# Two batches' projections moved to other steps in front of the 16-wide attention stages

## The chip, the cores and the metric

One core of a Trainium2 chip runs the whole kernel in one launch. The metric is device time in microseconds (us) for that launch. The engines are TensorE (PE, with its weight loads listed as PEld), VectorE (DVE), ScalarE (ACT), GpSimd (POOL) and SyncE (SP), which here only issues DMAs. "SPq" and "ACTq" are the DMA issues of SyncE and ScalarE.

## The reference

Eight layers act on x of shape (8, 256, 256), each as x + layer(layernorm(x)), in the order attention, FFN, attention, FFN and so on. The attentions read a second input ctx of the same shape. Layers 0 and 6 are the ones that the change touches. Both are the same computation with their own weights, 16 heads of width 16:

```python
qh = (q @ Wq.T + bq).reshape(B, Nq, 16, 16).transpose(0, 2, 1, 3)    # q = layernorm(x)
kh = (k @ Wk.T + bk).reshape(B, Nkv, 16, 16).transpose(0, 2, 1, 3)   # k = v = ctx
vh = (v @ Wv.T + bv).reshape(B, Nkv, 16, 16).transpose(0, 2, 1, 3)
attn = jax.nn.softmax(jnp.einsum('bhqd,bhkd->bhqk', qh, kh) * 0.25, axis=-1)
out = jnp.einsum('bhqk,bhkd->bhqd', attn, vh)
out = out.transpose(0, 2, 1, 3).reshape(B, Nq, 256) @ Wo.T + bo
```

The layers between them (a routed FFN, a 64-wide attention, a second FFN, an attention without heads, a quantised FFN) and the last layer (a block-quantised linear) are other functions of the kernel, which the change leaves alone.

## The kernel before, in words

`narrow_head_attention` (line 591) is called twice, as stage a0 and as stage a6. In the trace the names of both begin with `a_`: a0 lies at about 8 to 230 us of the span, a6 at about 1605 to 1840 us.

The work is cut into 64 pairs of heads, 8 for each of the 8 batches. A loop over a step number T is unrolled in each engine's program, from -14 to 87 or so; a pair's scores are computed at step T and its second, "shifted" scores at step T + 7 (`LAG`), where t = T - 7. Every engine walks through the same steps in the same order:

- PE at step T: first half of `scores_and_shifted` (line 776: one head's scores of pair T into `ps_s`, one head's shifted scores of pair t into `ps_t`), then the rounds that the list `EVENTS` (line 622) gives for T (`project`, line 726), then the second half, then at every second step the product with the values (`weighted_values`, line 807).
- DVE at step T: the maxima over the scores (`largest`, line 875), between its two halves its share of the rounds of step T - 1 (`read_round`), and for batch f at T = 8f - 14 the normalisation's statistics and at 8f - 13 its application (line 910 and 916), which waits for POOL's reciprocal root (`norm_rstd`, line 60).
- ACT at step T: its share of the rounds of step T - 1, `context_high(f)` at T = 8f - 9 (line 1033), then the exponentials of pair t (line 999), whose results PE waits for one step later, since the bank of shifted scores must be read before it is written again (line 792). The maxima go into the operand of the shifted scores by DMAs that ACT issues (`place_maxima`, line 972).
- SP: `place_unit(u)` (line 707), one for each unit of 4 pairs. It issues 6 DMAs for q and 6 for k of 64 KB, which lay the high and low parts of q and k out as the operands `qa` and `ka`. Unit 2f and 2f + 1 belong to batch f. PE waits for unit u at step T = 4u (line 783). `context(f)`, 2 DMAs that fetch a batch of ctx, stands in the same queue: `context(2)` right behind `place_unit(2)`, before `place_unit(3)` (line 719 to 722).
- POOL: a loop over the batches f: `norm_rstd(f)`, `context_low(f)`, `output_bias(f - 1)`, in this order (line 1074).

A round is one use of one of three PSUM banks: "hT" transposes the normalised input of a batch, "q", "k" and "v" are its projections (12 matmuls of 128 x 256 each), "mT", "OT", "BT" and "out" are transposes of maxima and outputs and the output projection. A round claims its bank once the round three places before it in the sorted list is consumed. The context's parts `ctx_hi` and `ctx_lo` have one buffer: `context_high(f)` waits until the values of batch f - 1 are projected (line 936).

Of the kernel before, what the change touches and what calls it, by code (L numbers as in the profile page):

```python
# [590 lines left out]
def narrow_head_attention(nc, chip, stage, w, prefetch, late=(), x_rest=()):  # L591
# [28 lines left out]
    STATS, APPLY, CTX = -14, -13, -9  # L620
    FIRST = STATS
    EVENTS = []
    for f in range(B):
        EVENTS += [(8 * f - 10, 0, "hT", f), (8 * f - 8, 0, "q", f), (8 * f - 6, 0, "k", f), (8 * f - 2, 1, "v", f), (8 * f + 20, 3, "out", f)]
    for u in range(NUNIT):
        EVENTS += [(4 * u + 4, 2, "mT", u), (4 * u + LAG + 6, 2, "OT", u), (4 * u + LAG + 8, 2, "BT", u)]
    EVENTS.sort()
# [4 lines left out]
    def rounds_at(s):  # L632
        return [(kind, n) for at, o, kind, n in EVENTS if at == s]

    def group_at(s):

        n, odd = divmod(s - LAG - PPG, PPG)
        return n if not odd and 0 <= n < NG else None

    with ExitStack() as ctx:  # L640
# [84 lines left out]
        def _(pe):  # L725
            def project(kind, n):
# [10 lines left out]
                elif kind in "qkv":  # L737
                    if n == 0:
                        pe.wait_ge(sem["W_lo"], "qkv".index(kind) + 1)
                    _, hi, lo = weights[kind]  # L740
                    if kind == "q":
                        pe.wait_ge(sem["hT_lo"], n + 1)
# [183 lines left out]
        def _(act):  # L926
            def weights_high(kind):
                W, hi, lo = weights[kind]
                if kind == "q":
                    nc.scalar.activation(hi[:, :, :], W, ACT.Copy, scale=SCALE).then_inc(sem["W_hi"], 1)  # L930
                else:
                    nc.scalar.copy(hi[:, :, :], W).then_inc(sem["W_hi"], 1)

            def context_high(f):
                act.wait_ge(sem["ctx"], 16 * KC * (f + 1))
                after(act, sem["vp"], f)
                nc.scalar.copy(ctx_hi[:, :, :], ctxT[:, :, :]).then_inc(sem["ctx_hi"], 1)
# [34 lines left out]
            def place_maxima(u, t):  # L972

                part, name = (m_hi, "m_hi") if t == 0 else (m_lo, "m_lo")
                act.wait_ge(sem[name], u + 1)
                if t == 0 and u >= RING:
                    act.wait_ge(sem["st"], 2 * PPU * (u - RING + 1))
                for i in range(2):
                    row = i * HALF + K1 + t
                    act.dma_start(qa[row:row + 1, u % RING, :, :].bitcast(F32),  # L980
                                  part[i * PPU:(i + 1) * PPU, u % 2, :].bitcast(F32)).then_inc(sem[f"mrow{u % 2}"], 16)
# [11 lines left out]
            def keep_output(n):  # L993

                act.wait_ge(sem["pv"], n + 1)
                after(act, sem["OTp"], (n - NO) // 2 + 1)
                nc.scalar.copy(osb[:, n % NO, :], ps_o[:, :]).then_inc(sem["osb"], 1)

            def exponentials(t, i):

                act.wait_ge(sem["st"], 2 * t + (1 - i) + 1)
                after(act, sem["pv"], (t - NPT) // PPG + 1)
                nc.scalar.activation(probT[:, t % NPT, i, :, :], ps_t[i][:, :, :], ACT.Exp).then_inc(sem["exp"], 1)  # L1003

            def read_round(kind, n):
                if kind == "hT":
                    hT_high(n)
                elif kind in "qk":
                    high_part(kind, n)
                elif kind == "v":  # L1010
                    keep_v(n)
                elif kind == "mT":
                    maxima_high(n)
                elif kind == "BT":
                    keep_oT(n)
# [7 lines left out]
            for T in range(FIRST, LAST + 1):  # L1023
                t = T - LAG
                if T == STATS:
                    weights_high("q")
                if T == APPLY:
                    weights_high("k")
                    weights_high("v")
                for this in rounds_at(T - 1):  # L1030
                    read_round(*this)
                for f in range(B):
                    if T == 8 * f + CTX:
                        context_high(f)
                if 0 <= t < NT:
                    exponentials(t, 1)
                for kind, n in rounds_at(T - 1):
                    if kind == "mT":
                        place_maxima(n, 0)
                if group_at(T - 1) is not None:  # L1040
                    keep_output(group_at(T - 1))
                if 0 <= t < NT:
                    exponentials(t, 0)
                for kind, n in rounds_at(T - 1):
                    if kind == "mT":
                        place_maxima(n, 1)
                if T == NPAIR:
                    loads = prefetch(act, sem["wload"])
# [1388 lines left out]
def build(nc, a, out):  # L2437
    with ExitStack() as ctx:
# [28 lines left out]
        with ExitStack() as st:  # L2467
# [11 lines left out]
            def _(pool):  # L2479
                nc.gpsimd.memset(chip.minus_half[:, :], -0.5).then_inc(sem["consts"], 1)  # L2480
                pool.wait_ge(sem["consts"], 1)


        stages = [lambda: narrow_head_attention(nc, chip, "a0", w0, fetch1, w0.late, [(chip.x[:, TB:2 * TB, :], x_tiles[:, TB:2 * TB, :]),
                                                                                               (chip.x[:, 2 * TB:, :], x_tiles[:, 2 * TB:, :])]),
                  lambda: expert_choice_ffn(nc, chip, "f1", w1, fetch2),
                  lambda: head_attention(nc, chip, "a2", w2, fetch3),
                  lambda: top2_experts(nc, chip, "f3", w3),
                  lambda: context_attention(nc, chip, "a4", fetch5),
                  lambda: quantised_ffn(nc, chip, "f5", w5, fetch6),  # L2490
                  lambda: narrow_head_attention(nc, chip, "a6", w6, fetch7),
                  lambda: block_quantised_linear(nc, chip, "f7", w7, out)]
        for stage in stages:
# [62 lines left out]
```

## Time and profile before

| | us |
|---|---|
| median of 3 runs | 1927.48 (1919.68 to 1937.14) |
| profiled execution | 1938.52 |
| its span in the trace | 1936.6 |

The span is the time from the first to the last recorded instruction; the rest of an execution's time, 1.9 us, lies around it. The three runs spread over 0.9% with nothing changed between them. All times of rows below are us from the span's start, unless marked ns.

### The profile page before, as it was taken

To read this page: it belongs to the slowest core of one execution; us is meant where nothing else is said; L and a number is where in the kernel's file an instruction comes from. 1 tells how busy PE (TensorE), PEld (TensorE's weight loads), DVE (VectorE), ACT (ScalarE), POOL (GpSimd) and SP (SyncE) were. 2 spreads that over 40 slices of the span, in tenths; PEclk is the share of its full clock that TensorE was granted. 3 is DMA by queue.
4 is the path that set the end of the run, shared out by engine and by line. 5 is a ranking of instruction groups with operands and counts; after the bars stand their busy time and mean duration, and the time that the engine had idled before them with its cause. 6 is when DMAs were issued, how large, how long until landed. Compare 5 with 4: busy or idle time off the path is not lost. (4 is left out here: it accounts for less than half of the span.)

```text
span 1936.6 us, 32029 instructions
## 1 busy us (share of the span) xinstructions
PE 1625.2 (84%) x10798; PEld 1359.1 (70%) x10798; DVE 1260.0 (65%) x2837; ACT 944.8 (49%) x2139; POOL 429.8 (22%) x429
## 2 busy tenths in 40 slices
PE   4899738999995799999999989999985996899815
PEld 3566427888885788988889868889874785666413
DVE  3677355656563878766787568766756754677297
ACT  1566524444343768766687644433433541566400
POOL 2111013656564312211122000000003312111022
PEclk7899879999998999999999989999997996799656
DMA  3322053464654100000000100000024002222001
GB/s 125 112 87 82 29 211 102 121 150 122 149 122 96 60 2 6 5 5 5 0 5 0 66 1 1 1 1 0 1 66 136 1 0 68 76 88 83 9 0 43
DMA packets 81169, 108.35 MB, mean 56 GB/s; under 512 B 13104, under 2 KB 75312, under 8 KB 78512
## 3 DMA queue, kind: packets, MB, share of 16 engines
q1 hardware_dynamic: 64256, 85.33, 13.2%
q0 software_dynamic: 12288, 16.79, 5.0%
q10 hardware_dynamic: 4528, 4.98, 0.8%
q8 instruction: 57, 0.93, 0.2%
q14 instruction: 40, 0.33, 0.1%
HBM read 66.68 MB, written 14.68 MB: 42 GB/s over the span
## 5 line engine op out<-in xcount | busy, mean ns | idle before, releaser
L881 DVE TENSOR_REDUCE a_nmax<-a_s 128x2 f32<-128x512 f32 x256 | 170.2, 687 | 119.4 <-PE a_s L796 118.9
L1003 ACT ACTIVATE a_probT<-a_t 128x512 f32<-128x512 f32 x256 | 151.3, 602 | 146.0 <-PE a_t L800 125.2
L317 PE MATMUL a_o<-a_probT,a_vb 128*128 128x128 f32 x1024 | 143.4, 284 | 28.2 <-ACT a_oT L525 27.5
L574 POOL TENSOR_TENSOR a_k_hi<-a_k_hi,a_k_lo 64x256 fp32r<-64x256 f32 x128 | 93.3, 729 | 328.7 <-ACT a_k_hi L501 319.2
L796 PE MATMUL a_s<-a_ka,a_qa 48*128 48x256 f32 x512 | 125.3, 351 | 39.7 <-DMA a_qa<-a_m_lo 14.9
L317 PEld LDWEIGHTS a_o<-a_probT,a_vb 128*128 128x128 f32 x1024 | 126.6, 194 | 44.6 <-issue 43.3
L796 PEld LDWEIGHTS a_s<-a_ka,a_qa 48*128 48x128 f32 x512 | 81.1, 210 | 99.0 <-issue 72.6
L514 ACT ACTIVATE a_prob<-a_score,a_nmax 128x256 f32<-128x256 f32 x256 | 119.4, 472 | 46.8 <-DVE a_nmax L421 45.5
L421 DVE TENSOR_REDUCE a_nmax<-a_score 128x2 f32<-128x512 f32 x128 | 88.4, 690 | 82.4 <-PE a_score L298 80.6
L800 PE MATMUL a_t<-a_qa,a_ka 50*128 50x256 f32 x512 | 124.2, 343 | 2.2 <-DMA a_qa<-a_m_lo 1.2
L1427 POOL DMA_INDIRECT x_rows<-f_hn,f_scatter_row x64 | 108.7, 1698 | 29.9 <-issue 19.0
L1384 ACT ACTIVATE f_gate<-f_gate 128x512 f32<-128x512 f32 x64 | 38.3, 599 | 150.6 <-PE f_gate L1216 129.2
L2111 PE MATMUL f_y<-area_odd_parts,f_y_hi 128*128 128x256 f32 x384 | 109.2, 284 | 0.0
L2277 ACT ACTIVATE f_relu<-f_u 128x512 f32<-128x512 f32 x96 | 57.2, 598 | 85.3 <-PE f_u L2099 84.8
L1315 DVE TENSOR_TENSOR f_y<-f_gate,f_value 128x512 f32<-128x512 f32 x64 | 44.1, 688 | 81.3 <-PE f_value L1216 81.3
L520 ACT COPY a_probT<-a_T 128x512 f32<-128x512 f32 x128 | 75.6, 590 | 41.5 <-PE a_T L306 38.6
L1228 PE MATMUL f_z<-area_odd_parts,f_y_hi 128*128 128x256 f32 x384 | 84.7, 287 | 9.0 <-DVE f_y_lo L1307 9.0
L63 POOL TENSOR_TENSOR a_rstd<-a_veps,minus_half 128x2 f32<-128x2 f32 x32 | 22.9, 716 | 305.7 <-DVE a_veps L57 305.7
L63 POOL TENSOR_TENSOR f_rstd<-f_veps,minus_half 128x4 f32<-128x4 f32 x12 | 12.1, 1011 | 345.5 <-DVE f_veps L57 345.5
L2209 DVE TENSOR_TENSOR f_y<-f_relu 128x512 f32<-128x512 f32 x96 | 65.1, 690 | 34.8 <-ACT f_relu L2277 32.1
L800 PEld LDWEIGHTS a_t<-a_qa,a_ka 50*128 50x128 f32 x512 | 78.2, 201 | 10.6 <-issue 5.1
L428 DVE TENSOR_SCALAR a_prob<-a_prob,a_rinv 128x256 f32<-128x256 f32 x256 | 80.2, 356 | 4.5
(329 smaller groups left out, 5080.8 us busy)
## 6 DMA issues: line engine op xcount, KB each, us to landing
area_odd<-in_L_experts SPq DMA_DIRECT2D x15, 1536.0 KB, 7.7
a_ctxT<-in_ctxT SPq DMA_DIRECT2D x64, 128.0 KB, 2.5
a_qa<-a_q_hi SPq DMA_DIRECT2D x128, 64.0 KB, 2.6
a_ka<-a_k_hi SPq DMA_DIRECT2D x128, 64.0 KB, 2.6
area_odd<-in_L_W SPq DMA_DIRECT2D x2, 3072.0 KB, 11.0
a_qa<-a_q_lo SPq DMA_DIRECT2D x64, 64.0 KB, 2.6
a_ka<-a_k_lo SPq DMA_DIRECT2D x64, 64.0 KB, 2.6
x_rows<-x_tok SPq DMA_DIRECT2D x1, 2048.0 KB, 7.6
```

The costliest lines, as they stand in the source:

```text
L317: last = nc.tensor.matmul(ps_o[:, :], vb[:, kc, hh[i] * P:(hh[i] + 1) * P], probT[:, u % 2, kc, i, :], start=(i == 0 and kc == 0), stop=(i ...
L421: nc.vector.tensor_reduce(nmax[:, u % NPROB, :], ps_score[u % NB][:, :, :], AX.X, ALU.max, negate=True).then_inc(sem["nmax"], 1)
L428: last = nc.vector.tensor_scalar(prob[:, u % NPROB, i, :], prob[:, u % NPROB, i, :], rinv[:, u % NPROB, i:i + 1], None, ALU.mult)
L514: last = nc.scalar.activation(prob[:, u % NPROB, i, :], ps_score[u % NB][:, i, :], ACT.Exp, bias=nmax[:, u % NPROB, i:i + 1], accum_out=rs ...
L574: nc.gpsimd.tensor_tensor(k_hi[other, h, :], k_hi[own, h, :].bitcast(F32), k_lo[own, h ^ 1, :].bitcast(F32), ALU.add).then_inc(sem["k_copy ...
L796: last_s = nc.tensor.matmul(ps_s[i][:, half, :], qa[rows, u % RING, j, half * P:(half + 1) * P], ka[rows, u % RING, j, :], start=True, sto ...
L800: last_t = nc.tensor.matmul(ps_t[o][:, half, :], ka[rows, v % RING, m, half * P:(half + 1) * P], qa[rows, v % RING, m, :], start=True, sto ...
L881: nc.vector.tensor_reduce(nmax[:, u % 2, :, i * PPU + j], ps_s[i][:, :, :], AX.X, ALU.max, negate=True).then_inc(sem["nmax"], 1)
L1003: nc.scalar.activation(probT[:, t % NPT, i, :, :], ps_t[i][:, :, :], ACT.Exp).then_inc(sem["exp"], 1)
L1228: last = nc.tensor.matmul(ps_z[s // 2][:, s % 2, :], h[:, f, s * P:(s + 1) * P], W[:, f, :], start=(f == 0 and i == 0), stop=(f == NF - 1 ...
L1427: nc.gpsimd.indirect_dma_start(chip.x_rows, bass.IndirectOffsetOnAxis(ap=scatter_row[:, q, s:s + 1], axis=0), z[:, q, s, :], None, compute ...
L2111: last = nc.tensor.matmul(ps_y[t // 2][:, t % 2, :], h[:, e % 2, f, t * P:(t + 1) * P], W, start=(f == 0 and i == 0), stop=(f == NF[e] - 1 ...
```

## The change

For batch 1, the q round goes from step 0 to step 4, the k round from step 2 to step 5. For batch 0, the v round goes from step -2 to step 2. `context_high(1)`, which must stand behind the values of batch 0, goes from step -1 to step 3. Since the rounds are sorted by step and then by a rank (q, k: 0; v: 1; mT: 2), the list around them goes from hT1, v0, q1, k1, mT0, hT2, v1 to hT1, v0, q1, mT0, k1, hT2, v1. Nothing else is edited, and it holds for both stages.

```diff
@@ -621,7 +621,8 @@
     for f in range(B):
-        EVENTS += [(8 * f - 10, 0, "hT", f), (8 * f - 8, 0, "q", f), (8 * f - 6, 0, "k", f), (8 * f - 2, 1, "v", f), (8 * f + 20, 3, "out", f)]
+        EVENTS += [(8 * f - 10, 0, "hT", f), (8 * f - 8 if f != 1 else 4, 0, "q", f), (8 * f - 6 if f != 1 else 5, 0, "k", f),
+                   (8 * f - 2 if f != 0 else 2, 1, "v", f), (8 * f + 20, 3, "out", f)]
     for u in range(NUNIT):
         EVENTS += [(4 * u + 4, 2, "mT", u), (4 * u + LAG + 6, 2, "OT", u), (4 * u + LAG + 8, 2, "BT", u)]
@@ -1030,7 +1031,7 @@
                 for f in range(B):
-                    if T == 8 * f + CTX:
+                    if T == (8 * f + CTX if f != 1 else 3):
                         context_high(f)
```

## Rows read from the trace of the kernel before

**Rows 1.** The page's busy time of one engine: us, share of the span, instructions.

```profile
PE 1625.2 (84%) x10798; PEld 1359.1 (70%) x10798; DVE 1260.0 (65%) x2837; ACT 944.8 (49%) x2139; POOL 429.8 (22%) x429
```

**Rows 2.** Windows: stretch, its length, busy us (instructions) by engine, granted PE clock, DMA.

```profile
core 0: us, PE busy (x) PEld busy (x) DVE busy (x) ACT busy (x) POOL busy (x), PEclk, DMA share, GB/s
31.60:52.70 21.10, 17.74 (x68) 14.19 (x68) 11.86 (x26) 2.63 (x6) 1.63 (x3) 0.50 0.26 85
52.70:81.20 28.50, 22.26 (x161) 15.35 (x160) 15.51 (x33) 12.53 (x26) 3.37 (x4) 0.74 0.40 130
1625.50:1646.65 21.15, 17.79 (x68) 14.22 (x69) 11.86 (x26) 2.63 (x6) 1.79 (x3) 0.50 0.27 90
1646.65:1675.30 28.65, 25.11 (x161) 17.59 (x160) 15.56 (x33) 13.64 (x27) 3.34 (x4) 0.62 0.24 75
```

**Rows 3.** Timeline of PE in a0: start, us, instruction, count [idle before, releaser].

```profile
31.57 0.76 PE L796 MATMUL a_s<-a_ka,a_qa 48*128 48x256 f32 x2 [2.94 <-DMA a_ka<-a_k_lo]
...
46.17 3.01 PE L796 MATMUL a_s<-a_ka,a_qa 48*128 48x256 f32 x8
...
55.10 0.35 PE L796 MATMUL a_s<-a_ka,a_qa 48*128 48x256 f32 x1 [0.29 <-DVE a_nmax L881]
```

**Rows 4.** Timeline of PE in a6, steps 0, 2, 8, 14 and 22.

```profile
1625.49 0.76 PE L796 MATMUL a_s<-a_ka,a_qa 48*128 48x256 f32 x2 [2.81 <-DMA a_ka<-a_k_lo]
...
1631.94 0.79 PE L752 MATMUL a_proj<-a_ctx_hi,a_Wk_hi 128*128 128x256 f32 x2
...
1634.80 0.80 PE L796 MATMUL a_s<-a_ka,a_qa 48*128 48x256 f32 x4
...
1649.91 0.35 PE L796 MATMUL a_s<-a_ka,a_qa 48*128 48x256 f32 x1 [1.18 <-ACT a_probT L1003]
...
1675.25 0.39 PE L796 MATMUL a_s<-a_ka,a_qa 48*128 48x256 f32 x1
...
1697.33 0.38 PE L796 MATMUL a_s<-a_ka,a_qa 48*128 48x256 f32 x1
```

**Rows 5.** Timeline of SP's issues in a0: q and k of unit 2, then the context.

```profile
38.04 1.19 SPq L704 DMA_DIRECT2D a_qa<-a_q_hi  x2
...
40.55 1.23 SPq L704 DMA_DIRECT2D a_qa<-a_q_hi  x2
44.94 2.46 SPq L704 DMA_DIRECT2D a_ka<-a_k_hi  x4
...
48.96 2.30 SPq L694 DMA_DIRECT2D a_ctxT<-in_ctxT  x2
```

**Rows 6.** The context tile, us from issue to landing: first in a0, then in a6.

```profile
DMA to landing us min/median/max: 3.3/3.5/3.7
...
DMA to landing us min/median/max: 2.5/2.7/3.0
```

**Rows 7.** Timeline of ACT in a0, step 7.

```profile
53.40 0.62 ACT L937 CAST a_ctx_hi<-a_ctxT 128x512 fp32r<-128x512 f32 x1
53.98 0.60 ACT L1003 ACTIVATE a_probT<-a_t 128x512 f32<-128x512 f32 x1
```

**Rows 8.** Timeline of ACT in a6, step 7.

```profile
1647.24 0.62 ACT L937 CAST a_ctx_hi<-a_ctxT 128x512 fp32r<-128x512 f32 x1
1647.88 1.28 ACT L1003 ACT_TABLE_LOAD   x1
1649.17 1.09 ACT L1003 ACTIVATE a_probT<-a_t 128x512 f32<-128x512 f32 x2
```

**Rows 9.** Timeline of DVE in a0, steps 1 to 4.

```profile
37.15 0.87 DVE L856 SCALAR_TENSOR_TENSOR a_q_lo<-a_proj,area_even,a_q_hi 128x256 fp32r<-128x256 f32 x2
...
41.70 0.69 DVE L881 TENSOR_REDUCE a_nmax<-a_s 128x2 f32<-128x512 f32 x1 [2.48 <-PE a_s L796]
...
43.45 0.69 DVE L881 TENSOR_REDUCE a_nmax<-a_s 128x2 f32<-128x512 f32 x1
...
45.43 0.73 DVE L70 TENSOR_SCALAR a_hn<-x_tok,a_mv,a_rstd 128x256 f32<-128x256 f32 x2
```

**Rows 10.** Timeline of POOL in a0: context's low part, output bias, reciprocal root.

```profile
29.90 1.26 POOL L1068 TENSOR_TENSOR a_ctx_lo<-a_ctxT,a_ctx_hi 128x512 fp32r<-128x512 f32 x1 [5.14 <-ACT a_ctx_hi L937]
31.12 1.41 POOL L1062 TENSOR_TENSOR x_tok<-x_tok,area_even 128x256 f32<-128x256 f32 x2
...
43.61 0.71 POOL L63 TENSOR_TENSOR a_rstd<-a_veps,minus_half 128x2 f32<-128x2 f32 x1 [11.09 <-DVE a_veps L57]
```

## Prediction

> **What bounds the kernel now.** I read the page first: PE is busy 84% of the span, more than any other engine [rows 1]. That is an average over eight stages; the change lives in the head of two of them, so I read those heads by stretches [rows 2]. In a0 the steps 0 to 6 (first scores up to the last matmuls without shifted scores) take 21.1 us, in a6 21.15 us, both at a granted clock of 0.50, which is the lower of TensorE's two levels, 1.2 GHz. The next eight steps (to the second half of step 14) take 28.5 and 28.65 us at mean clocks of 0.74 and 0.62. Later a batch of eight steps at full clock takes 1697.33 - 1675.25 = 22.1 us [rows 4]. So the head costs more per step than the rest, and half clock and waits are the two reasons.
>
> Then I read the timelines of each queue through steps 0 to 8, because the change moves rounds between queues that are in order. I set x = 0 at the first scores (31.57 in a0, 1625.49 in a6 [rows 3, 4]). Step 8 began at x = 23.5 in a0 and 24.4 in a6 [rows 3, 4]. In a6 the PE had waited 1.18 us for ACT's exponential there, and that exponential stood behind `context_high(2)` and a table load of 1.28 us [rows 8]; in a0 it also ran right behind `context_high(2)`, but no later than PE wanted it [rows 7]. That order on ACT is the thing to keep in mind: at step 7 ACT first takes the third batch of ctx and only then can read the first shifted scores.
>
> **What the change moves.** Nothing is added or removed: the same 36 matmuls for q1, k1 and v0, the same DVE, ACT and POOL work, the same DMAs, in another order. Everything follows from three shifts.
>
> *v0 from step -2 to step 2.* A projection at half clock costs 2.86 us of PE (1634.80 - 1631.94 [rows 4]). At step -2 it was covered by the wait for the placed operands (2.94 us idle in a0, 2.81 in a6 even after it [rows 3, 4]), so taking it away there gains nothing: step 0 is set by the DMAs of unit 0, and those by q0 and k0, which stay. At step 2 it lies where k1 lay, with the same price.
>
> *context_high(1) from step -1 to step 3.* POOL is in order, and `norm_rstd(2)`, for which DVE waits at step 3, stands behind `context_low(1)` and `output_bias(0)`. Both were long done; now they begin when v0 is projected. By rows: v0 ends at x = 6.4; ACT keeps v and casts ctx by 7.6 (two instructions of 0.6 [rows 7]); POOL needs 1.26 + 1.41 + 0.71 us [rows 10], to x = 11.0. DVE reaches that point at x = 10.3 (below). The new wait is 0.7 us; behind it stands the first maximum of step 4.
>
> *q1 and k1 from steps 0 and 2 to 4 and 5.* On PE the sum for steps 0 to 6 changes only by v0, 2.86 us, of which most fills gaps that PE has there (21.1 - 17.7 = 3.4 us idle [rows 2]). But q1 and k1 feed SP, and that queue has hardly any room. Working forward at half clock:
> - Two bare steps take 3.1 us (8 matmuls in 3.01 [rows 3]), so step 2 begins at 3.1, v0 runs from 3.6 to 6.5, the second maximum of step 2 begins at 7.35. The statistics follow and the next maximum begins 43.45 - 41.70 = 1.75 later [rows 9], at 9.1; the step's other maximum ends at 10.4, the application (0.73 [rows 9]) waits until 11.05 and ends at 11.8.
> - q1 runs on PE from 10.4 to 13.2, the transposes of the maxima take about 0.5 more; two maxima of step 4 and 5 then end at 15.85, and the low part of q1 (0.87 [rows 9]) is done at x = 16.65. Before, it was done at 38.02 - 31.57 = 6.5.
> - SP then issues q of unit 2. Six transfers take 40.55 + 1.23 - 38.04 = 3.74 us, the six for k 48.96 - 44.94 = 4.0 with the gaps [rows 5]. The low part of k1 is done at about 20.4, just as SP gets to it. So unit 2 is issued by x = 24.4 (before: 17.4), and the two DMAs of `context(2)` behind it by about 25.7. The second lands 2.7 us (a6) to 3.5 us (a0) after its own issue begins at 25.0 [rows 6]: x = 27.7 and 28.5. Before, it had landed by the time ACT came.
> - ACT at step 7 would be ready for it at about x = 22.6 and waits some 5 us. Queued behind it on ACT are all exponentials. The cast of 0.62 and the exponential of 0.60 [rows 7] give PE's step 8 in a0 at x = 29.7; with the 1.28 of the table load, which stands behind the cast [rows 8], in a6 at x = 30.3. Unit 2 itself lands at about 26.5, so it is hidden by this wait.
> - Unit 3 is issued by x = 33.4 and needed at step 12, which was at about 39 and is now later: hidden.
>
> Step 8 comes 29.7 - 23.5 = **6.2 us later in a0** and 30.3 - 24.4 = **5.9 us later in a6**. Behind step 8 the same work remains with PE the fullest engine, so I expect none of it back.
>
> **The clock.** In both stages before, the mean clock is 0.50 up to the start of step 7 and above it from there on, in a0 more (0.74) than in a6 (0.62) [rows 2]: behind the dense v1 it rose for a while. Now PE is idle for over 6 us between steps 7 and 8, and I take it to be at half clock for step 8's q2, 2.86 us. At full clock that is half, so a0, which had more of it, loses 1.4 and a6, where it held for less, some 0.5. The bounds: 0 in each if it has risen anyway; at most 2.5 in a0. I don't take more, since a6 went through these eight steps no slower than a0 although its clock was lower (28.65 and 28.5 [rows 2]): waits cover much of it.
>
> The Trainium skill, "TensorE: Matmul & The Clock Gate", Part 1, "What's actually happening", says that the clock is low by default and that activity releases it. By that rule packing q1, k1, v1 in front of the shifted scores should raise the clock earlier; that is the second rival below. The rows only show that a projection alone at steps 0 and 2 did not raise it and v1 did [rows 2].
>
> **Sum.** 6.2 + 5.9 + 1.4 + 0.5 = 14.0 us on the profiled execution's 1938.5, that is 0.72%. On the median shown, 1927.5, which is 0.6% below the profiled one, it gives 1941.4.
>
> **Rivals.**
> 1. *Slower by over 1%.* The stall leaves the clock low for more than step 8: if the eight steps after it, at present 28.5 us, or the next eight, run at half clock throughout. Eight steps take 22.1 us at full clock [rows 4] and about 28.6 at mostly half clock [rows 2], so each further batch at half clock costs 6.5 us in one stage. With one such batch the sum is +20.5 (1947.9). It decides from the point where the second batch's steps (14 on) stay at 0.5. Against: the clock rose at step 14 in both stages, and the dense hT3 and v2 are still there.
> 2. *Not slower: the packing does what it seems to be for.* If the clock rises during k1 or v1 and is high from step 8 to 14, these 6.5 steps take 17.9 us (6.5/8 x 22.1) instead of 25.3 (1675.25 - 1649.91 [rows 4]), which gives 7.4 back in each stage. The sum is 12.1 - 14.8 = -2.7, 1924.8. For: the eight steps do take 28.5 now. Against: the ACT wait comes between the packed rounds and those steps, and leaves PE idle for longer than the wait of 2.9 us before step 0, after which steps 0 to 6 ran at 0.50.
> 3. *The delay is smaller.* If q1 itself runs at full clock and POOL is not late, the low part of q1 comes at about x = 14.5 and each stage loses 2 us less: +10.0, 1937.4. I count it to the forecast.
>
> **How the numbers follow.** Forecast, +8 to +19 us: 0.70. Rival 1: 0.18. Rival 2 and everything else near zero: 0.12. The three runs before spread by 0.9%, so about 1% is what a measurement tells from no change; my forecast of 0.72% lies within it but near the edge, so a quarter of its upper half may be read as slower by over 1%. Chances: slower by over 1% 0.25, within 1% 0.72, faster 0.03. The range takes the forecast's bounds (+8 to +19) with 0.3% of scatter on the upper side, and reaches down to rival 2's side to no change: 1928 to 1953.
>
> **What would show it.** In the changed kernel's timeline: ACT's `a_ctx_hi` of step 7 with an idle stretch of some 5 us before it, ended by a DMA of `a_ctxT`; SP's q of unit 2 issued 16 to 17 us after the first scores; POOL's third `a_rstd` right behind `output_bias`, and a wait of DVE for it under 1.5 us; PE's step 8 at x = 29 to 31. The stretch of steps 0 to 6 should still be about 22 us at 0.50. I am wrong if step 8 comes at x below 27, if ACT finds the context landed, or if the clock is 1.00 through steps 8 to 13.

## The result, and the profile after

The changed kernel is slower: 1943.92 us median of 4 runs (1939.18 to 1947.70) against 1923.89 (1919.68 to 1937.14), ratio 1.0092 with a 95% interval of 1.0055 to 1.0130. (The two medians alone would give 1.0104, the means of the runs, 1943.7 and 1926.2, give 1.0091.) Measured again beside the last experiments it was 1.0077 (1.0050 to 1.0104). So it loses 0.8 to 0.9%, some 15 to 18 us.

The two profiled executions don't show that in their spans (1937.4 and 1936.6 us), because the one of before (1938.52 us) was slower than all of its timed runs and the one of after the fastest of its four. What they show is where the time goes in the two heads. I use x again, the time since a stage's first scores; they are at 31.15 in a0 and 1629.27 in a6. First PE's timeline of the changed kernel, in the columns of [rows 3]:

```profile
31.15 0.80 PE L797 MATMUL a_s<-a_ka,a_qa 48*128 48x256 f32 x4 [4.72 <-DMA a_ka<-a_k_lo]
...
50.75 0.50 PE L797 MATMUL a_s<-a_ka,a_qa 48*128 48x256 f32 x2
...
61.43 0.55 PE L797 MATMUL a_s<-a_ka,a_qa 48*128 48x256 f32 x1 [8.73 <-ACT a_probT L1004]
...
62.15 0.79 PE L753 MATMUL a_proj<-a_hT_hi,a_Wq_hi 128*128 128x256 f32 x2
...
1629.27 0.80 PE L797 MATMUL a_s<-a_ka,a_qa 48*128 48x256 f32 x4 [4.63 <-DMA a_ka<-a_k_lo]
...
1661.12 0.55 PE L797 MATMUL a_s<-a_ka,a_qa 48*128 48x256 f32 x1 [10.29 <-ACT a_probT L1004]
```

Step 8 begins at x = 30.3 in a0 and 31.8 in a6, where [rows 3, 4] gave 23.5 and 24.4. In front of it PE stands idle for 8.7 and 10.3 us, and what ends the idle time is ACT's exponential. So the next timeline is ACT's, at step 7, first in a0, then in a6 (compare [rows 7, 8]):

```profile
50.98 0.61 ACT L964 COPY a_vb<-a_proj 128x512 f32<-128x512 f32 x1
60.17 0.62 ACT L938 CAST a_ctx_hi<-a_ctxT 128x512 fp32r<-128x512 f32 x1 [8.58 <-DMA a_ctxT<-in_ctxT]
60.69 1.08 ACT L1004 ACTIVATE a_probT<-a_t 128x512 f32<-128x512 f32 x2
...
1658.45 0.62 ACT L938 CAST a_ctx_hi<-a_ctxT 128x512 fp32r<-128x512 f32 x1 [8.72 <-DMA a_ctxT<-in_ctxT]
1659.09 1.28 ACT L1004 ACT_TABLE_LOAD   x1
```

ACT waited 8.6 us for the third batch's context, with the exponentials behind it. The context is late because of SP's queue (a0, beside [rows 5]):

```profile
48.18 1.57 SPq L705 DMA_DIRECT2D a_qa<-a_q_hi  x2
49.80 1.67 SPq L705 DMA_DIRECT2D a_qa<-a_q_lo  x2
51.51 1.23 SPq L705 DMA_DIRECT2D a_qa<-a_q_hi  x2
52.78 2.50 SPq L705 DMA_DIRECT2D a_ka<-a_k_hi  x4
55.33 1.23 SPq L705 DMA_DIRECT2D a_ka<-a_k_lo  x2
56.60 1.06 SPq L695 DMA_DIRECT2D a_ctxT<-in_ctxT  x2
```

The queue stands still until q1's low part is done (x = 17.0; before 6.5), then issues 12 transfers and only then the two of the context. They land 2.5 to 2.9 us after their issue. Last the windows, for a0 and a6: steps 0 to 6 up to the end of v1, as in the first and third of [rows 2]; the idle stretch before step 8; steps 8 to 14.

```profile
core 0: us, PE busy (x) PEld busy (x) DVE busy (x) ACT busy (x) POOL busy (x), PEclk, DMA share, GB/s
31.15:50.75 19.60, 16.85 (x80) 13.80 (x80) 11.33 (x25) 3.14 (x8) 3.29 (x4) 0.58 0.12 41
52.60:61.40 8.80, 0.10 (x2) 0.00 (x1) 1.49 (x3) 1.23 (x3) 0.54 (x1) 0.60 0.36 119
61.40:86.90 25.50, 24.22 (x150) 16.45 (x150) 13.02 (x29) 10.64 (x23) 2.82 (x4) 0.54 0.39 136
1629.27:1648.57 19.30, 16.54 (x80) 13.48 (x81) 11.24 (x24) 2.82 (x7) 3.29 (x4) 0.59 0.13 44
1650.70:1661.10 10.40, 0.13 (x4) 0.01 (x1) 1.37 (x3) 2.62 (x4) 1.96 (x3) 0.55 0.36 119
1661.10:1681.20 20.10, 17.02 (x150) 12.27 (x150) 12.93 (x29) 10.54 (x23) 1.38 (x2) 0.89 0.26 81
```

Two things are to be seen. With the projections packed the clock of the head was higher, 0.58 and 0.59 instead of 0.50 (0.72 and 0.59 in a second trace, run 12): steps 0 to 7 are done by x = 21.5, before by 23.2, with one projection more in them. And it bought nothing, since the next 9 to 10 us are idle.

### The profile page after: what moved, and what is told of

The parts are those of the page before. It is cut to its first block and busy times, and to the rows that moved or that the text cites. A ratio compares the mean times of both kernels' runs of the same rounds, so it can differ in the third digit from the quotient of the medians.

```text
span 1937.4 us, 32029 instructions
## 1 busy us (share of the span) xinstructions
PE 1605.9 (83%) x10798; PEld 1345.5 (69%) x10798; DVE 1260.4 (65%) x2837; ACT 943.5 (49%) x2139; POOL 430.4 (22%) x429
## 5 line engine op out<-in xcount | busy, mean ns | idle before, releaser
L797 PE MATMUL a_s<-a_ka,a_qa 48*128 48x256 f32 x512 | 122.2, 343 | 58.2 <-ACT a_probT L1004 25.3
L317 PE MATMUL a_o<-a_probT,a_vb 128*128 128x128 f32 x1024 | 143.4, 284 | 28.0 <-ACT a_oT L525 27.2
L514 ACT ACTIVATE a_prob<-a_score,a_nmax 128x256 f32<-128x256 f32 x256 | 119.3, 472 | 46.9 <-DVE a_nmax L421 45.5
L63 POOL TENSOR_TENSOR f_rstd<-f_veps,minus_half 128x4 f32<-128x4 f32 x12 | 12.1, 1011 | 338.5 <-DVE f_veps L57 338.5
```

The lines of the kernel that those rows point to most:

```text
L317: last = nc.tensor.matmul(ps_o[:, :], vb[:, kc, hh[i] * P:(hh[i] + 1) * P], probT[:, u % 2, kc, i, :], start=(i == 0 and kc == 0), stop=(i ...
L514: last = nc.scalar.activation(prob[:, u % NPROB, i, :], ps_score[u % NB][:, i, :], ACT.Exp, bias=nmax[:, u % NPROB, i:i + 1], accum_out=rs ...
L797: last_s = nc.tensor.matmul(ps_s[i][:, half, :], qa[rows, u % RING, j, half * P:(half + 1) * P], ka[rows, u % RING, j, :], start=True, sto ...
```

## Experiments

Each kernel was timed against the kernel before on the same chip. For each of them x of step 8 is read from the trace as above. The table stands first, since the edits below are told by it; "sum" is the shift of step 8 in both stages against 23.5 and 24.4, and the column behind it is that sum over 1927 us.

| kernel | step 8, a0 | a6 | sum, us | sum, % | ratio measured (95%) |
|---|---|---|---|---|---|
| changed | 30.3 | 31.8 | +14.2 | +0.74 | 1.0092 (1.0055 to 1.0130) |
| changed, again | 29.2 | 31.6 | +12.9 | +0.67 | 1.0077 (1.0050 to 1.0104) |
| 1 changed, context first | 26.7 | 27.2 | +6.0 | +0.31 | 1.0041 (1.0015 to 1.0068) |
| 2 changed, q1 back at 0 | 28.5 | 31.3 | +11.9 | +0.62 | 1.0073 (1.0044 to 1.0102) |
| 3 only q1 moved | 28.2 | 31.2 | +11.5 | +0.60 | 1.0069 (1.0040 to 1.0098) |
| 4 before, context first | 23.5 | 24.4 | 0 | 0 | 0.9999 (0.9974 to 1.0025) |
| 5 before, context late | 30.9 | 30.9 | +13.9 | +0.72 | 1.0066 (1.0039 to 1.0093) |
| 6 only v0 moved, to step 0 | 22.8 | 26.1 | +1.0 | +0.05 | 1.0024 (0.9998 to 1.0051) |
| 7 packed earlier, context first | 24.7 | 24.0 | +0.8 | +0.04 | 1.0012 (0.9989 to 1.0034) |
| 8 changed, cast behind | 27.1 | 27.1 | +6.3 | +0.33 | 1.0040 (1.0013 to 1.0066) |
| 9 before, extra matmuls ahead | 21.1 | 21.3 | -5.5 | -0.29 | 0.9983 (0.9957 to 1.0009) |
| 10 as 9, and in the steps | 22.5 | 22.1 | -3.3 | -0.17 | 0.9961 (0.9939 to 0.9984) |
| 11 as 7, with extra matmuls | 23.8 | 23.2 | -0.9 | -0.05 | 1.0027 (1.0008 to 1.0047) |

In every row but the last the shift of step 8 lies within the interval of the measured ratio. It doesn't in run 11.

**1. The context ahead of unit 2.** My theory is the queue: ACT's wait for a context that SP issues late. The rivals are the moved values with the POOL chain, and the clock. This edit of the changed kernel takes only the lateness of the context away:

```diff
+            context(2)
             for u in range(2, NUNIT):
                 place_unit(u)
-                if u % UPB == 0 and u // UPB + 1 < B:
+                if u % UPB == 0 and 2 < u // UPB + 1 < B:
                     context(u // UPB + 1)
```

> The changed kernel with one edit: context(2) is issued ahead of unit 2 on the SP queue instead of behind it. If the loss is ACT's wait for the third batch of ctx, that wait (8.6 us in both stages of the changed kernel) goes, and step 8 waits for the placement of unit 2 instead: it begins at x = 26 to 27 after the first scores (30.3 and 31.9 in the changed kernel, 23.5 and 24.4 before), and the ratio to before falls from 1.009 to about 1.004. If the loss is the values of batch 0 at step 2 or the late low part of ctx, step 8 stays at 30 or later and the ratio stays at 1.009.

Measured: step 8 at 26.7 and 27.2, ratio 1.0041. PE's row of step 8 in a0 names another releaser now, the placement of unit 2:

```profile
58.26 0.55 PE L798 MATMUL a_s<-a_ka,a_qa 48*128 48x256 f32 x1 [5.95 <-DMA a_ka<-a_k_lo]
```

So about half of the loss is the context (8.2 of 14.2 us at step 8), and behind it stands a second wait from the same queue, 3 us later than the old step 8.

**2. q1 back at step 0.** An edit of the changed kernel:

```diff
-        EVENTS += [..., (8 * f - 8 if f != 1 else 4, 0, "q", f), ...
+        EVENTS += [..., (8 * f - 8, 0, "q", f), ...
```

> The changed kernel with q of batch 1 back at step 0; k stays at 5 and the values of batch 0 at 2. SP can then issue q of unit 2 early, but its k part still waits for k1. By the queue theory the low part of k1 comes 2 to 3 us earlier than in the changed kernel because q1 is no longer in front of it on PE, so the six k DMAs and context(2) end at about x = 23, and step 8 begins at x = 27 to 29: most of the loss stays, ratio about 1.005 to 1.008. A theory in which the clock or q1's place at step 4 is the cause has it back at 1.000.

Measured: 28.5 and 31.3, ratio 1.0073. a6 is later than I expected, a0 within the range. But k1 came no earlier, although I had reasoned that it would: in a0 SP issued the first k of unit 2 at x = 20.3 (51.70 - 31.39) and ended the context at 25.1, not 23. With q of unit 2 issued early the late k alone holds most of the delay, 11.9 of 14.2 us. DVE still waited 0.9 us for the reciprocal root here.

**3. Only q1 moved.** k1, v0 and the cast of batch 1 are where they were before.

```diff
-        EVENTS += [..., (8 * f - 8, 0, "q", f), ...
+        EVENTS += [..., (8 * f - 8 if f != 1 else 4, 0, "q", f), ...
```

> Only q of batch 1 moved to step 4; k at 2, values of batch 0 at -2 and the ctx cast at -1 as before. SP issues q before k of the unit, so the queue theory has its twelve DMAs and context(2) all behind q1 again: the low part of q1 at about x = 14 to 17, step 8 at x = 27 to 30, ratio 1.005 to 1.009 with nothing of the POOL chain moved. If the values at step 2 and the POOL chain are what costs, this one is within 0.2% of before and DVE doesn't wait for the reciprocal root.

Measured: 28.2 and 31.2, ratio 1.0069. One projection of one batch, moved by four steps, costs most of what the whole change costs. In its trace DVE comes to q1's low part at x = 15.3 (46.49 - 31.21) and ACT waits for the context (ACT's timeline, a0):

```profile
58.16 0.62 ACT L938 CAST a_ctx_hi<-a_ctxT 128x512 fp32r<-128x512 f32 x1 [7.62 <-DMA a_ctxT<-in_ctxT]
```

DVE's application at step 3 follows the maximum before it with no wait for POOL, so the POOL chain is no part of this loss. Runs 2 and 3 together also say why one late projection is enough: SP takes q before k, so a late q1 holds back all 12 transfers and the context, and a late k1 alone still holds back six of them and the context.

**4. Control: the kernel before with the context first.** The diff of run 1 on the kernel before.

> Control: the kernel before with the same reordering of the SP queue as in the first run (context(2) ahead of unit 2). There context(2) had landed in time, so nothing is to be gained: step 8 at x = 23 to 25 and a ratio within 0.4% of 1. context(2) now waits for the low part of batch 1's ctx, which is done before the first scores, so it delays unit 2 by its own two issues (1.3 us), which is hidden unless unit 2 is needed sooner than I read it. It also gives a second trace of what is nearly the kernel before, to see how much the clock's rise and fall differs between two executions.

Measured: 23.5 and 24.4, exactly as before, ratio 0.9999. The order in the queue is free as long as the queue is early. The trace served as a second look at the kernel before; its windows from step 8 to 14, a0 and a6:

```profile
54.60:76.50 21.90, 17.49 (x148) 11.89 (x148) 14.03 (x31) 10.72 (x23) 2.43 (x4) 0.84 0.45 152
1645.80:1669.00 23.20, 20.08 (x148) 14.31 (x148) 13.20 (x30) 10.74 (x24) 1.59 (x3) 0.74 0.25 74
```

The same steps took 26.1 and 25.3 us in the first execution. PE has the same instructions in both, only two DMAs stand elsewhere in SP's queue, so I put the difference of up to 4 us in one stage to where the clock rises. One trace can't price anything that depends on it. Step 8 came out alike.

**5. The suspected wait alone.** All rounds of the kernel before stay, only `context(2)` goes behind unit 3:

```diff
             for u in range(2, NUNIT):
                 place_unit(u)
-                if u % UPB == 0 and u // UPB + 1 < B:
+                if u == UPB + 1:
+                    context(2)
+                if u > UPB and u % UPB == 0 and u // UPB + 1 < B:
                     context(u // UPB + 1)
```

> The kernel before with the suspected wait alone: context(2) is issued behind unit 3 instead of in front of it, every round stays at its old step. ACT's cast at step 7 then finds the context late. By the queue theory the second DMA lands at about x = 31, step 8 begins at x = 32 in a0 and 33 in a6 (23.5 and 24.4 before), a little later than in the changed kernel (30.3 and 31.8), and the ratio to before is 1.008 to 1.011 although q1, k1 and the values of batch 0 have not moved. If the moved rounds themselves cost the time, this stays within 0.3% of before.

Measured: 30.9 in both, ratio 1.0066. It came 1 us earlier than expected in a0 and 2 us in a6, and the ratio is below my 1.008. The rows of a0, SP's issue, ACT's wait and PE's, show the pattern of the changed kernel without any moved round:

```profile
57.60 1.06 SPq L694 DMA_DIRECT2D a_ctxT<-in_ctxT  x2
...
60.64 0.62 ACT L939 CAST a_ctx_hi<-a_ctxT 128x512 fp32r<-128x512 f32 x1 [7.76 <-DMA a_ctxT<-in_ctxT]
...
61.90 0.55 PE L798 MATMUL a_s<-a_ka,a_qa 48*128 48x256 f32 x1 [7.63 <-ACT a_probT L1005]
```

**6. Only v0 moved**, to step 0 and not to 2 as in the change, with batch 1's cast at step 1. (At step 2, v0 would be sorted behind k1, which reads the context for which v0 must first release the buffer.)

```diff
-        EVENTS += [..., (8 * f - 2, 1, "v", f), ...
+        EVENTS += [..., (8 * f - 2 if f != 0 else 0, 1, "v", f), ...
-                    if T == 8 * f + CTX:
+                    if T == (8 * f + CTX if f != 1 else 1):
```

> The kernel before with only the values of batch 0 on the path: from step -2 to step 0, the ctx cast of batch 1 to step 1; q at 0 and k at 2 as before. This prices the moved values by themselves: 2.86 us of PE at half clock less what falls in gaps. I predicted 0.8 us at the end of step 6; so step 8 at x = 24 to 26, and a ratio of 1.000 to 1.002. If the values cost their full price in both stages, step 8 is at 26.4 and 27.3 and the ratio is 1.003.

Measured: 22.8 and 26.1, the first below and the second just above the expected 24 to 26; ratio 1.0024 with an interval from 0.9998 to 1.0051. It can't be told from nothing, nor from the full price of 0.3%. (The 0.8 us that the expectation names stands nowhere in the prediction, which has only "most of which fills gaps".) Run 7, which has v0 at step 2 and the cast at step 3, says a little more: there step 8 came 0.8 us late in both stages together.

**7. Packed earlier.** The changed kernel with the diff of run 1, q1 at step 3 and k1 at step 4.

> The changed kernel with context(2) ahead of unit 2 as in the first run, and q and k of batch 1 at steps 3 and 4 instead of 4 and 5, so that the three projections are still close together but SP gets its work some 3 us earlier. By the queue theory the low part of k1 comes at x = 16 to 17, unit 2 lands at about 23, and step 8 is no longer later than before (x = 23 to 25): ratio within 0.3% of 1. If packing the projections raises the clock early enough to be of use, step 14 comes earlier than in the kernel before (49.6 and 49.8 there) and the ratio falls below 1, to 0.997 or so. If the values at step 2 cost by themselves, it stays at 1.003.

Measured: 24.7 and 24.0, ratio 1.0012. This is the change as it might have been meant: three projections close together, but with SP's work coming early enough. PE's row of step 8 in a0:

```profile
55.82 0.55 PE L798 MATMUL a_s<-a_ka,a_qa 48*128 48x256 f32 x1 [4.18 <-DMA a_ka<-a_k_lo]
```

The delay is gone and no gain has come: the head ran at a mean clock of 0.68 in both stages, but PE still waits 4.2 us in a0 for the placed k, so the higher clock is spent on arriving earlier at a transfer. Step 14 came at x = 49.3 and 45.7; the kernel before had 49.6 and 49.8, run 4 had 45.4 and 47.6, so the trace shows no gain either.

**8. Who stands behind the wait.** In the changed kernel only ACT's order is edited. Its cast of batch 2 goes behind the exponentials of step 7:

```diff
                 for f in range(B):
-                    if T == (8 * f + CTX if f != 1 else 3):
+                    if T == (8 * f + CTX if f != 1 else 3) and f != 2:
                         context_high(f)
...
                 if 0 <= t < NT:
                     exponentials(t, 0)
+                if T == 2 * 8 + CTX:
+                    context_high(2)
```

> The changed kernel with ACT's order alone edited: the cast of the third batch's context stands behind the two exponentials of step 7 instead of in front of them; SP's queue is as in the changed kernel. This takes away who is queued behind the wait, not the late DMA. Expected: the context still lands at x = 28 to 29, but PE's step 8 no longer waits for it; unit 2's placement is next (26 to 27), and the wait moves to the exponentials of step 8, which now stand behind the cast (x = 29 to 30). So step 8 at 26.5 to 27.5, step 9 at about 30, and a ratio between the first run's 1.004 and 1.007.

Measured: 27.1 in both, ratio 1.0040. ACT's row and PE's in a0:

```profile
60.00 0.62 ACT L938 CAST a_ctx_hi<-a_ctxT 128x512 fp32r<-128x512 f32 x1 [6.57 <-DMA a_ctxT<-in_ctxT]
...
58.37 0.55 PE L797 MATMUL a_s<-a_ka,a_qa 48*128 48x256 f32 x1 [5.60 <-DMA a_ka<-a_k_lo]
```

The context is as late as ever and ACT still waits 6.6 us for it, but step 8 no longer does. The place of the wait in ACT's order made it cost. What is left, 6.3 us at step 8, is the same wait for unit 2's placement as in run 1; run 7, where q1 and k1 come a step earlier, is without most of it.

**9. The clock without moving anything.** The kernel before with 12 extra matmuls behind step -4 and 12 behind step -1. Their result is never read; the computation is complete.

```diff
                 for this in rounds_at(T):
                     project(*this)
+                for _ in range({-4: 12, -1: 12}.get(T, 0)):
+                    nc.tensor.matmul(ps_o[:, :], W_hi[0][:, 0, 0:P], W_hi[0][:, 0, :], start=True, stop=True)
```

> The kernel before with 24 extra matmuls of 128x256 whose result is overwritten unread (12 behind step -4, 12 behind step -1), put into the two idle stretches of PE of some 3 us before the first scores. They add 2.6 us each at half clock, 1.4 at full clock. This asks whether the clock of steps 0 to 6 can be had without moving any projection. If PE stays at full clock to step 2 or beyond, each of q1, k1, v1 costs 1.4 us less and step 8 comes 3 to 5 us earlier than 23.5 and 24.4: ratio 0.995 to 0.998. If the clock falls all the same once PE waits for DVE between scores, the ratio is within 0.2% of 1.

Measured: step 8 at 21.1 and 21.3, that is 2.4 and 3.1 us earlier where I had 3 to 5, with the head at 0.72 and 0.65; ratio 0.9983 (0.9957 to 1.0009). The mechanism shows, less than hoped; the ratio alone doesn't settle it.

**10. The same inside the steps too**: `{-4: 12, -1: 12, 1: 3, 3: 3, 4: 2, 5: 3}`.

> As the run above, with 11 further such matmuls inside steps 1, 3, 4 and 5, in the gaps in which PE waits for the maxima. If the clock then stays up through steps 0 to 6, step 8 begins at x = 18 to 20 (SP's queue sets it then: unit 1 is issued by 5.5, unit 2 by about 13 and context(2) by 14.5, landing at 17) and the ratio is 0.993 to 0.997. If it stays at half clock, the extra matmuls cost 2.3 us in each stage: ratio 1.002.

Measured: ratio 0.9961 (0.9939 to 0.9984), faster than the kernel before and than the changed one. The ratio is in the expected range, but step 8, by which I had reasoned, is at 22.5 and 22.1, not at 18 to 20, and later than in run 9. Windows of its steps 0 to 6 and 7 to 14, a0 and a6:

```profile
31.02:51.18 20.16, 17.69 (x79) 14.52 (x80) 11.93 (x26) 2.73 (x6) 0.82 (x2) 0.62 0.30 98
51.18:76.54 25.36, 22.17 (x159) 15.76 (x158) 15.35 (x33) 12.67 (x26) 3.35 (x4) 0.69 0.39 133
1624.56:1643.44 18.88, 15.88 (x80) 12.60 (x80) 11.93 (x26) 2.84 (x6) 1.77 (x3) 0.73 0.32 104
1643.44:1666.34 22.90, 17.94 (x159) 12.87 (x159) 15.41 (x33) 13.63 (x27) 3.34 (x4) 0.92 0.25 84
```

Beside [rows 2] the head's clock is 0.62 and 0.73 instead of 0.50. In a6 the following steps ran at 0.92, above the 0.62 of the kernel before and the 0.71 of run 4; in a0 they ran at 0.69, below the 0.74 and 0.83 of these two. Step 8 accounts for 0.17% of the 0.39%. The rest is either in such clocks or scatter, and runs 9 and 10 can't be told apart: their intervals overlap, and their steps 14 came at x = 43.5 and 44.5, and 45.5 and 41.8.

**11. Both together**, run 7 with `{-4: 12, -1: 24, 0: 3, 1: 3}`.

> The early packed version (context(2) first, q and k of batch 1 at steps 3 and 4) with 42 extra unread matmuls before step 0 and in steps 0 and 1. If what holds the packed version at 1.001 is the low clock of its first steps, this one begins step 8 at x = 20 to 22 and its ratio is 0.995 to 0.998; if it is the placement of unit 2 behind k1, it stays at 1.000.

Measured: 23.8 and 23.2, ratio 1.0027 (1.0008 to 1.0047). A miss: the head's clock did rise, from 0.68 in run 7 to 0.77 and 0.76, and step 8 came 0.9 and 0.8 us earlier than there, but PE still waited 3.8 us in a0 for the placed k, and nothing was gained. The ratio is above both of my cases and above what step 8 gives; why is not shown.

**12. The changed kernel again.**

> The changed kernel once more, to have its ratio on the same chip as these and a second trace. The shift of step 8 in its first trace, 6.8 and 7.4 us, is 14.2 us or 0.74% if nothing of it is lost or given back later; the first measurement said 0.92% (0.55 to 1.30). Expected: 1.007 to 1.009, step 8 at x = 30 and 31.8, and the step 8 to 14 stretch anywhere between 20 and 26 us, as the clock falls out.

Measured: 29.2 and 31.6, ratio 1.0077, within the expected range. Steps 8 to 14 took 25.7 and 20.2 us, as in the first trace (25.5 and 20.1). Step 8 in a0 came 1.0 us earlier than there, with k1 all at full clock and the head at 0.72.

## Why the prediction was right

**The main path held step by step.** DVE's q1 low part was forecast for x = 16.65 and was done at 17.0; DVE waited 0.88 us for the reciprocal root where I had 0.7. These are the changed kernel's rows of DVE in a0:

```profile
42.59 0.74 DVE L70 TENSOR_SCALAR a_hn<-x_tok,a_mv,a_rstd 128x256 f32<-128x256 f32 x2 [0.88 <-POOL a_rstd L63]
...
47.28 0.87 DVE L857 SCALAR_TENSOR_TENSOR a_q_lo<-a_proj,area_even,a_q_hi 128x256 fp32r<-128x256 f32 x2
...
50.66 0.88 DVE L857 SCALAR_TENSOR_TENSOR a_k_lo<-a_proj,area_even,a_k_hi 128x256 fp32r<-128x256 f32 x2 [0.53 <-ACT a_k_hi L955]
```

k1's low part was forecast for 20.4 and done at 20.4, but that is luck: half of k1 ran at full clock, and then ACT came to k's high part only at 49.79, since it had been issuing the maxima until 49.69. It decided nothing, since SP came to k at 52.78.

That ACT would wait for the context, and that the exponentials stand behind it, is shown three ways: the wait alone makes the loss (run 5), taking the lateness away halves it (run 1), and taking the queued work from behind it halves it as well (run 8). That q1 acts through SP and not through POOL is shown by run 3, where DVE has no wait for POOL. For k1 it is the rows of run 2 that say it, in which SP stands still from q of unit 2 to k1's low part; DVE's short wait for POOL is still in that run.

**The term that was too small is the queue.** I had step 8 at 29.7 and 30.3 (the terms for a6 add up to 30.2), that is +6.2 and +5.9. It was +6.8 and +7.4 in the first trace, +5.7 and +7.2 in the second, 13.5 us in the mean instead of 12.1. From the first to the end of the last of the 14 issues SP took 9.5 us in a0 (57.66 - 48.18) where I had 9.0; in a6 it took 9.9, since one pair took 2.48 us instead of 1.23. The longer issues lie beside ACT's issues of the maxima or just behind them; what makes them long is not shown (see the last section). In a6 the context landed at x = 29.2 where I had 27.7.

**The clock came out otherwise.** I had taken half clock for all of steps 0 to 6. It rose during k1, so PE came to step 6's last scores at x = 19.6 and 19.3, where it had been 21.2 before and I had taken the stretch at about 22 us. It changed nothing at step 8, which the queue sets; ACT's wait was 8.6 us instead of 5, since ACT was ready at x = 20.4 and not 22.6 and the context landed at 29.0. The two small terms for step 8's q2 (+1.4 and +0.5) had the right picture, half clock at 62.15 in a0. From its first matmul to the transposes behind it q2 took 2.73 us in both stages and both traces of the changed kernel. In the kernel before it took 1.50 and 1.92, in run 4 1.50 and 2.73, so the two terms measure +2.0 together, or +1.2.

**"I expect none of it back" was wrong in a6.** There steps 8 to 14 took 20.1 and 20.2 us in the two traces of the changed kernel, at 0.89 and 0.88, against 25.3 in the kernel before and 23.2 in run 4: 3 to 5 us of the 7.4 are back by step 14. In a0 the same steps took 25.5 and 25.7 against 26.1 and 21.9. At step 14 the two traces of the changed kernel are 11 us behind the two of the old order in the mean, not 13.5. The total (14.0 us forecast, 15 to 18 measured, with intervals of 5 to 7 us to either side) agrees to 0.1 to 0.2%; the mechanism up to step 8 earns most of that, but how close the number came is in part luck.

**The rivals.** "Not slower" was half right: the clock does rise earlier, 0.58 and 0.59 instead of 0.50 in the head, and a6 ran at 0.89 behind step 8. It failed at the point named in the prediction, the wait between the packed rounds and the steps that should profit. Run 7 shows that with the context in time the packing still gives nothing that can be measured. "Slower by over 1%" is within the first interval as a number, but its mechanism did not occur: no second batch stayed at half clock, steps 14 to 22 took 22.1 and 22.6 us.

## What to carry to other kernels

When a piece of work is moved, follow what it feeds, not only what it costs: here the 12 matmuls of q1, which had room on TensorE, held back 12 DMA issues 0.64 us apart, and what stood last in that queue, a prefetch for another engine, was the thing that came late. A prefetch should be issued ahead of work that waits for something (run 1 against the changed kernel), and a wait for a prefetch should stand behind the work that others need at once (run 8). Before moving work to keep TensorE's clock up, unread matmuls in the idle gaps are worth a try: they move no other queue, and were the only edit here that gained, by 0.4% with 0.16% as the near end of the interval (run 10). With fewer of them the gain was not clear of noise (run 9), and on the packed kernel there was none (run 11).

## What the runs showed of the hardware

One issue of a 64 KB transfer mostly took SP 0.59 to 0.60 us, and the next began 0.64 us after it. Some took longer: pairs of 1.57, 1.67 and 2.48 us instead of 1.23 in the changed kernel. These lie beside ACT's issues of the maxima or up to 0.1 us behind them. But in a6 the pair at 1646.31 took 1.19 us although ACT issued beside it, and the kernel before has pairs of 1.77 us (at 64.54) and 1.95 us (at 1650.45) with no issue of ACT beside them. The cause stays open.

The Trainium skill, "DMA: Bandwidth & Descriptors", section "Issuing engines are not separate DMA queues", says that issuing from several engines saves only the sequencer's time, usually small beside the transfer. For one transfer the traces agree, with 0.6 us to issue and 2.5 to 2.9 us from the issue of the context to its landing. In a row the issues add up: 14 took 9.5 us on SP.

In a6 the exponential behind the table load of 1.28 us began 0.01 us after its end (1659.09 + 1.28, next at 1660.38).

Runs of unchanged code spread by 0.9 to 1.0%, and the traces show where within these two stages: from step 14 to step 54 a stage took 109.3 to 110.3 us in all 14 traces and both stages, but steps 8 to 14 took 21.9 or 26.1 us in a0 for the old order of rounds (at 0.84 and 0.74), and the end of a stage, from step 54 to the last shifted scores, 36.2 to 44.6 us. Even the same kernel, traced twice, had 0.58 and 0.72 as the clock of a0's head. So a claim on the clock needs several traces or a ratio over many runs.
